# Attention with keys, slot weights and gated rows turned by VectorE squares and DMA instead of TensorE

## The reference, cut to what matters

```
q, k = x@Wq, x@Wk  (64 per head);  v, g = x@Wv, x@Wg  (128 per head);  s = clip(x@Ws)  (64 slots per head)
z = cumlogsumexp(s);  p_t = exp(s_t - z_t);  decay_t = exp(z_{t-1} - z_t)
hk_t = hk_{t-1}*decay_t + k_t (x) p_t;   ok_t = (q_t/8) . hk_t;   pv_t = softmax(ok_t)
hv_t = hv_{t-1}*decay_t + p_t (x) v_t;   o_t = pv_t . hv_t
out = x + (rmsnorm(o)*gnorm * silu(g)) @ Wo
```

## Time and profile before

| | us |
|---|---|
| median of 3 runs | 2107.34 |
| the profiled execution, its own time | 2111.22 |
| its span, first to last instruction | 2109.5 |
| PE busy | 1982.6 (94%) |
| VectorE busy | 1365.2 (65%) |
| ScalarE busy | 669.6 (32%) |
| GpSimd busy | 278.8 (13%) |
| attention without its first and last stretch, 497 to 1537 us | 1040 |

### The profile page before, as it was taken

The page is one execution under the profiler, slowest core; times in us unless marked ns, Lnnn a source line. Parts: engine busy times, 40 slices in busy tenths (PEclk is TensorE's granted clock), DMA queues, the critical chain, the costliest instruction groups (busy, mean ns, idle before and its releaser), DMA issues. The chain is left out here.

```text
span 2109.5 us, 29738 instructions
## 1 busy us (share of the span) xinstructions
PE 1982.6 (94%) x11848; PEld 1629.8 (77%) x11848; DVE 1365.2 (65%) x2702; ACT 669.6 (32%) x1207; POOL 278.8 (13%) x216
## 2 busy tenths in 40 slices
PE   2999999969999999999999999999999689999998
PEld 1788888847888888888888888888887468888786
DVE  5765667736667666666766666666767766665684
ACT  2443445514222131221222221221212144443562
POOL 3110111011011020120110110210201200110100
PEclk9999999979999999999999999999999889999999
DMA  6463436660010010010000100100100155443565
GB/s 219 131 199 120 136 119 180 204 195 9 1 38 9 1 38 8 9 31 9 21 25 1 38 9 1 38 8 1 38 1 21 40 169 191 130 110 110 150 187 183
DMA packets 54329, 165.04 MB, mean 78 GB/s; under 512 B 5424, under 2 KB 5424, under 8 KB 54192
## 3 DMA queue, kind: packets, MB, share of 16 engines
q1 hardware_dynamic: 46736, 145.80, 21.1%
q0 software_dynamic: 7456, 17.34, 4.0%
HBM read 137.40 MB, written 25.72 MB: 77 GB/s over the span
## 5 line engine op out<-in xcount | busy, mean ns | idle before, releaser
L1227 PE MATMUL at_pj<-at_w_lo,at_xT_hi 128*128 128x512 f32 x512 | 210.5, 411 | 0.0
L1227 PE MATMUL at_pj<-at_w_hi,at_xT_lo 128*128 128x512 f32 x512 | 202.3, 395 | 0.0
L1227 PE MATMUL at_pj<-at_w_hi,at_xT_hi 128*128 128x512 f32 x512 | 202.3, 395 | 0.0
L1201 PE MATMUL at_pj<-at_xT_hi,at_w_lo 128*128 128x512 f32 x384 | 158.4, 412 | 7.6 <-DVE at_gate L1004 4.9
L550 DVE TENSOR_TENSOR last_ff_w_lo<-last_ff_stage,last_ff_w_hi 128x1024 fp32r<-128x1024 f32 x80 | 97.9, 1224 | 90.4 <-ACT last_ff_w_hi L373 90.2
L1201 PE MATMUL at_pj<-at_xT_hi,at_w_hi 128*128 128x512 f32 x384 | 152.3, 397 | 0.0
L1201 PE MATMUL at_pj<-at_xT_lo,at_w_hi 128*128 128x512 f32 x384 | 151.4, 394 | 0.0
L933 ACT ACTIVATE at_ok<-at_ok 128x512 f32<-128x512 f32 x32 | 20.3, 633 | 412.2 <-DVE at_ok L1122 412.2
L550 DVE TENSOR_TENSOR first_ff_w_lo<-first_ff_stage,first_ff_w_hi 128x1024 fp32r<-128x1024 f32 x80 | 97.9, 1224 | 77.7 <-ACT first_ff_w_hi L373 76.3
L840 POOL TENSOR_TENSOR at_coef<-at_ms,minus_half 128x4 f32<-128x4 f32 x64 | 63.5, 1008 | 559.8 <-DVE at_ms L1164 559.8
L825 POOL TENSOR_TENSOR at_w_lo<-at_stage,at_w_hi 128x1024 fp32r<-128x1024 f32 (+1 forms) x36 | 78.1, 2170 | 380.3 <-ACT at_w_hi L879 380.3
(11 more groups left out here) (315 smaller groups left out, 4783.7 us busy)
## 6 DMA issues: line engine op xcount, KB each, us to landing
first_ff_stage<-wff SPq DMA_DIRECT2D x90, 512.0 KB
last_ff_stage<-wff SPq DMA_DIRECT2D x90, 512.0 KB, 3.9
at_stage<-watt SPq DMA_DIRECT2D x24, 512.0 KB, 3.7
at_stage<-watt SPq DMA_DIRECT2D x16, 384.0 KB, 3.2
xres<-x SPq DMA_DIRECT2D x4, 1024.0 KB, 9.8
mid_rows<-xres SPq DMA_DIRECT2D x4, 1024.0 KB
out<-xres SPq DMA_DIRECT2D x4, 1024.0 KB
first_ff_xg<-sorted_rows SPq DMA_DIRECT2D x3, 1028.0 KB, 5.4
```

The source lines that it names most:

```text
L1201: last = pe.matmul(PJ[(7 * k + part) % 2][:, :], wq(w, kk, part), x[:, kk, tok], start=(kk == 0 and n == 0), stop=(kk == KC - 1 and n == 2))
L1227: last = pe.matmul(PJ[(7 * k + 3 + t) % 2][:, :], x[:, kk, tok], wvg(w, kk), start=(kk == 0 and n == 0), stop=(kk == KC - 1 and n == 2))
```

## The change

Units after the first no longer turn anything for kn, en and u on TensorE, except the last unit's u. VectorE transposes 32x32 squares in place of whole tiles (`dve.transpose`), four instructions of 128x512 a unit: kT and eT into `ke_blocks`, and u in two halves onto itself. SyncE then moves the squares to their places with 16 transfers for keys and slot weights together and 16 for u; each moves from 32 partitions to 32 partitions 8 runs of 32 numbers (128 bytes) a partition. kn and en are two halves of one tensor `turned_ke`. u lands in `u_moved`, which lies where uT_lo lies; ScalarE takes the high part from there, VectorE the low part, in place.

Orders change with it. TensorE: q, k, key-state, scores, value-state products, `project_s`, the read of hk, then `project_out` of the unit before. `project_out` uses banks R0 and R3. VectorE: `add_out` stands after the scaled read, `z_scan` before the masks, gates 2 and 3 ahead of the transposes of u. SyncE: the loads of weight pieces stand between the moves. Some routing scratch moves to dead memory (`dead_rows`).

```diff
         def _(sp):
...
+            def move_blocks(unit):
+                sp.wait_ge(blocks_done, 4 * unit - 2)
+                sp.wait_ge(dv_mm, unit)
+                squares = ke_blocks[:, :, :].rearrange("j n (c b i) -> j n c b i", b=SQUARES, i=SQUARE)
+                for a in range(SQUARES):
+                    for b in range(SQUARES):
+                        sp.dma_start(turned_ke[b * SQUARE:(b + 1) * SQUARE, :, :, a * SQUARE:(a + 1) * SQUARE],
+                                     squares[a * SQUARE:(a + 1) * SQUARE, :, :, b, :]).then_inc(ke_landed, 16)
+            def move_u(unit):
+                sp.wait_ge(blocks_done, 4 * unit + 4)
+                sp.wait_ge(wo_mm, unit * UC + 1)
+                squares = u[:, :, :, :].rearrange("p c h (b i) -> p (c h) b i", b=SQUARES)
+                for a in range(SQUARES):
+                    for b in range(SQUARES):
+                        sp.dma_start(u_moved[b * SQUARE:(b + 1) * SQUARE, :, :, a * SQUARE:(a + 1) * SQUARE].rearrange("p c h i -> p (c h) i"),
+                                     squares[a * SQUARE:(a + 1) * SQUARE, :, b, :]).then_inc(u_landed, 16)
+            load(0, 0, 0, 4)
+            for i in range(PAIRS):
+                for k in range(UNITS):
+                    if k == UNITS - 1 and i < PAIRS - 1:
+                        load(i + 1, 0, i + 1, 4)
+                    if i * UNITS + k + 1 < PAIRS * UNITS:
+                        move_blocks(i * UNITS + k + 1)
+                    if k == 0 and i < PAIRS - 1:
+                        load(i, 1, i + 1, 0)
+                    if k == UNITS - 2 and i < PAIRS - 1:
+                        load(i, 2, i + 1, 1)
+                        load(i, 3, i + 1, 2)
+                    if i * UNITS + k + 1 < PAIRS * UNITS:
+                        move_u(i * UNITS + k)
+                    if k == UNITS - 2 and i < PAIRS - 1:
+                        load(i, 4, i + 1, 3)
...
         def _(act):
...
                     if more:
                         q_scale(i, k + 1)
+                    if (i, k) != (0, 0):
+                        before = i * UNITS + k - 1
+                        act.wait_ge(u_landed, (before + 1) * SQUARES * SQUARES * 16)
+                        act.wait_ge(wo_mm, before * UC + 1)
+                        for b in range(2):
+                            act.activation(u_half(uT_hi, b), u_half(u_moved, b), ACT.Copy).then_inc(u_hi, 1)
+                    if more:
+                        e_exp(i, k + 1)
...
         def _(dve):
...
+            def k_squares(i, k):
+                dve.wait_ge(k_out, count(i, k, 1, 1))
+                dve.transpose(ke_blocks[:, 0, :], kT[:, :]).then_inc(blocks_done, 1)
+            def e_squares(i, k):
+                dve.wait_ge(e_done, count(i, k, 1, 1))
+                dve.transpose(ke_blocks[:, 1, :], eT[:, k % 2, :]).then_inc(blocks_done, 1)
...
                     dve.reciprocal(rzT[:, :], zT[:, :]).then_inc(rz_done, 1)
-                    if (i, k) != (0, 0):
-                        add_out(*((i, k - 1) if k else (i - 1, UNITS - 1)), last_pair and k > 0)
...
+                    if (i, k) != (0, 0):
+                        for b in range(2):
+                            dve.wait_ge(u_hi, count(i, k, 2, b - 1))
+                            dve.tensor_tensor(u_half(uT_lo, b), u_half(u_moved, b), u_half(uT_hi, b).bitcast(F32), ALU.subtract).then_inc(u_lo, 1)
+                    if more:
+                        k_squares(i, k + 1)
+                        s_clip(i, k + 1)
+                    dve.wait_ge(ok_mm, count(i, k, 1, 0))
+                    dve.wait_ge(rz_done, count(i, k, 1, 1))
+                    dve.tensor_tensor(pT[:, :], R[2][:, :], rzT[:, :], ALU.mult).then_inc(ok_scaled, 1)
+                    if more:
+                        e_squares(i, k + 1)
+                    if (i, k) != (0, 0):
+                        add_out(*((i, k - 1) if k else (i - 1, UNITS - 1)), last_pair and k > 0)
...
+                    if more:
+                        gate_make(i, k + 1, 2)
+                        gate_make(i, k + 1, 3)
                     for b in range(2):
-                        if more and b == 1:
-                            gate_make(i, k + 1, 2)
...
+                        if more:
+                            dve.wait_ge(u_done, count(i, k, 2, b + 1))
+                            dve.transpose(u_half(u, b), u_half(u, b)).then_inc(blocks_done, 1)
...
         def _(pe):
...
                         project_q(i, k + 1)
-                    if (i, k) != (0, 0):
-                        project_out(*((i, k - 1) if k else (i - 1, UNITS - 1)), True)
-                    if more:
                         project_k(i, k + 1)
-                    pe.wait_ge(en_out, count(i, k, 1, 1))
-                    pe.wait_ge(kn_out, count(i, k, 1, 1))
+                    if (i, k) == (0, 0):
+                        pe.wait_ge(ek_out, 2)
+                    else:
+                        pe.wait_ge(ke_landed, (i * UNITS + k) * SQUARES * SQUARES * 16)
...
                     last.then_inc(dv_mm, 1)
+                    if more:
+                        project_s(i, k + 1)
                     pe.wait_ge(hk_done, i * HK_AT[UNITS] + HK_AT[k + 1] + 1)
...
                     last.then_inc(ok_mm, 1)
-                    if more:
-                        project_s(i, k + 1)
+                    if (i, k) != (0, 0):
+                        project_out(*((i, k - 1) if k else (i - 1, UNITS - 1)))
...
-                    if more:
-                        turn_ek(i, k + 1)
```

More of the change, by code:

```diff
@@ L712, in phase_attention @@
         sem = lambda n: top.enter_context(nc.semaphore(n))
+        with nc.sbuf_tensor("at_dead_rows", [P, KC, TOK], F32) as dead_rows:
+            pass
         xT_hi = sb("at_xT_hi", [P, KC, TOK], F32R)
@@ L732, in phase_attention @@
         pT = sb("at_pT", [P, UNIT])
-        u = sb("at_u", [P, 2, UC, DV])
-        uT_hi = sb("at_uT_hi", [P, 2, 2, 2 * P], F32R)
-        uT_lo = sb("at_uT_lo", [P, 2, 2, 2 * P], F32R)
+        u = sb("at_u", [P, UC, 2, DV])
+        uT_hi = sb("at_uT_hi", [P, UC, 2, P], F32R)
+        with nc.sbuf_tensor("at_u_moved", [P, UC, 2, P], F32) as u_moved:
+            pass
+        uT_lo = sb("at_uT_lo", [P, UC, 2, P], F32R)
         highest = sb("at_highest", [P, 2 * UC])
@@ L1066, in add_out @@
                     dve.wait_ge(wo_mm, count(i, k, UC, cc + 1))
-                    dve.tensor_tensor(xres[:, k * UC + cc, :], R[2 + cc % 2][:, :], xres[:, k * UC + cc, :], ALU.add).then_inc(added, 1)
+                    dve.tensor_tensor(xres[:, k * UC + cc, :], R[3 * (cc % 2)][:, :], xres[:, k * UC + cc, :], ALU.add).then_inc(added, 1)
                     if with_statistics:
@@ L1143, in pair @@
                         gate_make(i, k + 1, 1)
-                        z_scan(i, k + 1)
                     if last_pair and k > 0:
@@ L1347, in pair @@
                         project_vg(i, k + 1, 0)
+                    pe.wait_ge(added, count(i, k, UC, 0))
                     pe.wait_ge(pv_done, count(i, k, 1, 1))
@@ L1383, in pair @@
                         pe.matmul(rt_total, c["ones"][:], routing["is1"][:, tiles(k - 1)], start=True, stop=True).then_inc(rank_mm, 1)
-                    for b in range(2):
-                        pe.wait_ge(u_done, count(i, k, 2, b + 1))
-                        for h in range(2):
-                            for a in range(2):
-                                last = pe.transpose(R[4 + b][:, (2 * h + a) * P:(2 * h + a + 1) * P], u[:, h, 2 * b + a, :], c["ident"][:])
-                        last.then_inc(u_tr, 1)
-                    if more:
-                        turn_ek(i, k + 1)
-                    else:
-                        project_out(i, k, False)
+                    if not more:
+                        for b in range(2):
+                            pe.wait_ge(u_done, count(i, k, 2, b + 1))
+                            for n, (cc, h) in enumerate(((2 * b, 0), (2 * b, 1), (2 * b + 1, 0), (2 * b + 1, 1))):
+                                last = pe.transpose(R[4 + b][:, chunk(n)], u[:, cc, h, :], c["ident"][:])
+                            last.then_inc(ek_tr, 1)
+                    if not more:
+                        project_out(i, k)
             for i in range(PAIRS):
```

97 lines of the change are left out of this document (45 added, 52 removed).

## The result

The changed kernel takes 2241.89 us (2239.41 to 2243.58) against 2108.31 (2104.89 to 2111.34) of the kernel before in the same comparison: ratio 1.0633, 95% interval 1.0613 to 1.0653. It is slower by 134 us; forecast were 2083, 24 us faster than before, and 2236 as the price of the second rival. The profiled execution took 2243.58 us, its span 2241.9; the difference of the spans is 132.4 us.

The account below looks back on a forecast made before the run. TensorE, busy 94% of the span, was taken as the bound; 30 units x (2.4 - 1.3) = 33, less 5 and 4, gave 24 us off: 2087 from the profiled execution, 2083 against the median. Range for 8 in 10: 2042 to 2270.

Parts of the forecast that it names:

- the second rival: Short runs set the pace of u's moves, 33 to 40 ns each: 2236 to 2290 us; chance 33%.
- What bounds, and the gain at q: TensorE bounds attention; turns and gate wait before the next q go, gaining 2.4 us a unit with nothing late.
- VectorE: Four added 128x512 transposes at 0.676 us each, 1.9 us more a unit; u's squares done at T + 2.5.
- T: Moment the last matmul of project_vg 3 gives way, when the next unit could begin; 678.69 in the earlier timeline.
- The issues: SyncE's 16 transfers of u at 0.428 us per issue: last issue at T + 9.0, landing at T + 11.0.
- one rival only: Gain given back by small lateness: issues of 0.5 us, landing at T + 12.1, about 2115 us; chance 11%.
- What lateness costs: At project_out, u 0.5 us late plus 0.9 at the third tile for add_out: 1.3 to 1.4 us a unit.
- The trip and the reads: About 2.0 us fixed from issue to landing, then reads until the first project_out matmul at T + 12.3.
- The price of a run: A 128-byte run in the DMA engines: taken as at most 27 ns, so issues set the pace; upper bound 80 ns.
- point of decision: Landing of u at about T + 12.1, from which the move decides for a slower kernel.
- Places of their own: About 5 us lost in the last unit, and 4 us in 7 bare waits for the weight piece.
- What would show it: Signs of being wrong: DMA share above 0.5 with landings beyond T + 12, clock under 0.95, or q waiting for a gate.

Follow-up runs that it names:

- e5: The new order of the engines' work alone, with keys, slot weights and u all turned by TensorE as before: 2078.66 us, ratio 0.9862 to the kernel before.
- e3: Changed kernel with u turned by TensorE again, keys and slot weights left to squares and 16 transfers: 2052.75 us, ratio 0.9745 to the kernel before.
- e9: Changed kernel with u sent through HBM by 4 stores and 1 load instead of 16 transfers: 2106.98 us, ratio 0.9994 to the kernel before.
- e2: Changed kernel with u's 16 transfers shared out, 9 from SyncE's queue and 7 from ScalarE's: 2097.12 us, ratio 0.9952 to the kernel before.
- e1: Changed kernel with 16 matmuls, results thrown away, put into the stop ahead of project_out: 2213.88 us, ratio 1.050 to the kernel before.
- e4: Changed kernel with the keys' and slot weights' transfers in six shapes by unit, results partly wrong; issue medians 591 to 622 ns, kernel time says nothing.
- e8: Changed kernel with other kinds of transfers (HBM or SBUF ends, spaced issues) for keys and slot weights by unit; issues 0.42 to 0.60 us, kernel time says nothing.

## Why the prediction was wrong, point by point

- *What bounds, and the gain at q.* Right. The q starts without a turn or a wait. e5 and e3 split the 2.34: 16 turns 1.66 us, of them 0.80 for u. The gain booked, 2.4, left out most of the wait for hk: it is 2.34 + 0.29 = 2.6 in the timeline, and 2.7 in the means (36.61 before, 34.72 - 0.80 = 33.92 with nothing late).
- *VectorE.* Right: the squares cost 0.65 to 0.71 us each (0.676 taken), u's were done at T + 2.5. VectorE's work grew from 679.07/1040 x 36.6 = 23.9 us a unit to 736.28/1160 x 40.8 = 25.9, 2.0 more (1.9 forecast). The price came from another operation of the same shape, and that held.
- *The issues: the step that turned the forecast gain into a loss.* "15 of them put the last issue at T + 2.6 + 6.4 = T + 9.0", with 0.428 us from the earlier trace rows. The row is a store into HBM; these transfers have both ends in SBUF and are 0.67 us apart, so the last was issued at 709.6, T + 12.6. The longest row, 0.522, had been my other end for one rival only; the true price lay outside both. I bounded the run's price from both sides and took the issue's from one row of another kind, without asking what differs.
- *What lateness costs: a second step that failed, behind the first.* The forecast says that u at T + 11.0 costs 1.3 us a unit and leaves 2083. e9 and e2 have u there at T + 10.9 and T + 10.7 in the mean, with the clock low in only a few units, and took 2107 and 2097. So with the issues priced rightly and made quicker the forecast gain would still not have come. In e9 `project_out` begins 0.95 us later than in e3 (mean, T + 12.39 against T + 11.44) and takes 1.09 longer (6.76 against 5.67); 0.5 and 0.9 had been taken, and 1.3 went into the sum. With 0.2 elsewhere a unit of e9 is 36.18 - 33.92 = 2.3 us longer than one with nothing late. Work ahead of `project_out` is done sooner (T + 11.4) than the T + 11.8 taken, so u is later for it; and u's landing moves from unit to unit, which costs where it is late and brings nothing where it is early. The last two units, with 5.7 us of waiting for uT_lo in e9, take most of what is left.
- *The trip and the reads.* Right: 1.9 us (the row of the keys' transfers) where I took 2.0, then 1.6 to TensorE's first matmul (711.57 to 713.14), where I took 1.3.
- *The price of a run.* The side taken was right. The page of before has this row of the first queue (packets, MB, share):

```profile
q1 hardware_dynamic: 46736, 145.80, 21.1%
```

  269,824 packets more, in (0.291 x 2241.9 - 0.211 x 2109.5) x 16 = 3317 us of engines: 12 ns each, under the 27 from which they would have set the pace. The rule of the Trainium skill on 512 B ("DMA: Bandwidth & Descriptors", "Specifications") gave 40 ns by my estimate; the measurement decides against that estimate, for transfers within SBUF.
- *The second rival* hit the time, 2236 for 2242, by luck: by another mechanism (runs at 12 ns, not 33) and with errors that cancel. It took a landing at T + 13.0; for the T + 14.6 that came its own terms give 4.1 + 0.9 + 3 - 2.4 = 5.6 a unit, about 2284. Too dear was its second cost, 3 us of clock and 0.9 for `add_out` one on top of the other: the two together were 2.35 in the unit shown, because the half clock covers the wait for `add_out`, which shows wherever the clock stays at 1.00 (e1, e2, e9: 0.8). That a low clock follows such stops was right. The length of the stop alone doesn't say when, though: in e2 a stop of 1.93 us was followed by 3.4 us at 0.50, and one of 2.65 us by none. Its point of decision, a landing at T + 12.1, was too late: e9, with T + 10.9, is already level with the kernel before.
- *Places of their own.* The wait for the weight piece: 4.2 us in 7 waits, 4 forecast. The last unit waited 6.7 us for uT_lo and is 8.9 us longer than before (from the last gate tile of the unit ahead to the end of attention, 54.0 against 45.1), 5 forecast.
- *What would show it.* Of the signs I had named for "wrong", the landing beyond T + 12 and the clock of 0.93 came; the DMA share above 0.5 did not (0.26 to 0.32). Read together they point at the queue, which e2 confirmed.

## What to carry to other kernels

Price the issue of a DMA by a row with the same kind of ends and about as many runs, and multiply by the count before anything else: sixteen small transfers to do one job were 10.7 us of a queue here. Two queues (e2) or fewer transfers (e9) took most of the loss back, but neither paid against leaving u on TensorE (2097 and 2107 against 2053). What a transfer replaces sets its worth: the 0.8 us that u's turns take of TensorE's queue can't pay for a trip of 11 or 14 us that TensorE then waits for, while keys and weights, needed much later, gain by the same means. A forecast that has data arrive about when it is needed should price the spread of arrivals and what queues up behind them, not only the mean. And a stop of some us on TensorE can cost more than its idle time: here 1.15 us of half clock behind 4.2 of idle time, in the mean.

## What the runs showed of the hardware

- An issue of a DMA from SBUF to SBUF takes 0.59 to 0.62 us of SyncE's queue (medians), whatever the shape between 32 and 256 runs (e4, e8), and 0.63 of ScalarE's (e2). With one end in HBM it takes 0.42 to 0.43 for 32 or 128 runs (e8), 0.33 for a load of 128 partitions x 4 KB and 0.68 for a store of 1024 runs of 128 B (e9).
- A run of 128 B within SBUF costs about 12 ns of a DMA engine. Stores of 1024 such runs into HBM, 0.69 us apart, hold the engines at a share of 0.96 with 165 GB/s.
- A 128x512 fp32 transpose in squares of 32 takes VectorE 0.65 to 0.71 us, as an elementwise operation of that shape.
- TensorE's clock fell to 0.50 some 2.7 us into its stop of 4.58 us and stayed there for the first 5 us of work behind it; `project_out` took 7.94 us. With the gap filled by matmuls nobody reads (e1) the clock stayed at 1.00 and it took 6.65.
